# A decoder's wide attention: row maxima from bf16 copies of keys and queries instead of the fp32r parts

## The reference

```python
q = (x_normed @ w_q)              # 1024 x 1024, 16 heads of 64
k, v = split(ctx @ w_kv)          # 6404 x 1024 each
scores = einsum('bhqd,bhkd->bhqk', q, k) * 64 ** -0.5
out = einsum('bhqk,bhkd->bhqd', softmax(scores), v) @ w_out + b_out
```

## Time and profile before

| | |
|---|---|
| three timed runs | 3840.88, 3855.21, 3857.26 us, median 3855.21 |
| profiled execution, span from first to last instruction | 3852.1 us |
| PE, DVE, ACT, POOL busy | 93%, 71%, 56%, 61% |
| first part of the wide attention | about 1607 to 1664 us |
| its steps | from 1664 us to about 3667 us |
| time of the profiled execution beyond its span | not given by the page |

### The profile page before, as it was taken

The page is one execution under the profiler, slowest core; times in us unless marked ns, Lnnn a source line. Parts: engine busy times, 40 slices in busy tenths (PEclk is TensorE's granted clock), DMA queues, the critical chain, the costliest instruction groups (busy, mean ns, idle before and its releaser), DMA issues.

```text
span 3852.1 us, 61024 instructions
## 1 busy us (share of the span) xinstructions
PE 3585.8 (93%) x23264; PEld 1471.9 (38%) x23264; DVE 2721.2 (71%) x4447; ACT 2164.0 (56%) x2535; POOL 2367.2 (61%) x1280
## 2 busy tenths in 40 slices
PE   6868999999999999889999999999999999999999
PEld 2332222222222244334444444444444444444444
DVE  5758888888888547776766666667666676666742
ACT  4667888888888744644444444444444444444422
POOL 3115656566565303047888888888788888889810
PEclk7969999999999999999999999999999999999999
DMA  4220001010001002500111000101010010012100
GB/s 132 52 44 8 1 10 27 1 26 11 1 1 43 10 5 87 204 14 25 29 29 29 27 28 27 30 25 32 26 29 27 28 29 28 25 55 71 30 0 6
DMA packets 74058, 126.73 MB, mean 33 GB/s; under 512 B 9875, under 2 KB 26341, under 8 KB 73093
## 3 DMA queue, kind: packets, MB, share of 16 engines
q1 hardware_dynamic: 73772, 122.82, 11.2%
HBM read 88.15 MB, written 34.64 MB: 32 GB/s over the span
## 4 chain that ended last, share of the span: by engine, by line
PE 51%; DVE 4%; ACT 2%; issue 1%; DVEq 0%; ACTq 0%
PE PS L2371 20%; PE PS L2345 12%; PE PS L2300 6%; PE PS L2358 5%; PE PS L2318 3%; DVE att_top_piece L2555 2%; DVE att_k_lo L2569 2%; PE PS L340 1%; PE PS L348 1%; PE PS L341 1%; ACT att_k_hi L2463 1%; PE PS L2311 0%; PE PS L2329 0%; PE PS L2323 0%; DVE att_prob L2535 0%
## 5 line engine op out<-in xcount | busy, mean ns | idle before, releaser
L2220 POOL TENSOR_TENSOR att_total<-att_total,att_prob 128x1024 f32<-128x1024 f32 x597 | 1543.7, 2586 | 352.4 <-ACT att_prob L2484 304.5
L2484 ACT ACTIVATE att_prob<-PS 128x1024 f32<-128x1024 f32 x816 | 790.9, 1021 | 1005.1 <-PE PS L2358 1005.1
L2555 DVE TENSOR_REDUCE att_top_piece<-PS 128x1 f32<-128x512 f32 (+1 forms) x1560 | 971.8, 664 | 349.6 <-PE PS L2300 339.8
L1878 DVE TENSOR_REDUCE att_top_piece<-PS 128x1 f32<-128x512 f32 (+1 forms) x1459 | 904.9, 664 | 132.4 <-PE PS L1591 127.0
L1781 ACT ACTIVATE att_prob<-PS 128x1024 f32<-128x1024 f32 (+2 forms) x912 | 892.0, 1004 | 173.5 <-PE PS L1623 170.6
L2371 PE MATMUL PS<-att_prob,att_vals 128*64 128x512 f32 x3264 | 792.0, 605 | 3.7 <-issue 2.9
L1646 PE MATMUL PS<-att_prob,cross_Vst 128*32 128x256 f32 (+1 forms) x5544 | 506.5, 431 | 2.7 <-issue 0.8
L1493 POOL TENSOR_TENSOR att_stage<-att_stage,att_run 128x512 f32<-128x512 f32 x150 | 191.4, 1276 | 401.9 <-ACT att_stage L1760 401.6
L2300 PE MATMUL PS<-att_k_hi,att_q_hi 64*128 64x512 f32 (+1 forms) x1664 | 376.3, 449 | 60.3 <-DVE att_top_piece L2555 47.0
L1591 PE MATMUL PS<-cross_Kstack,cross_Qmax 49*128 49x512 bf16 (+1 forms) x1664 | 323.5, 386 | 95.1 <-DVE att_top_piece L1878 33.4
L2345 PE MATMUL PS<-att_q_hi,att_k_hi 64*128 64x512 f32 x1632 | 329.1, 396 | 0.0
(11 more groups left out here) (316 smaller groups left out, 3394.6 us busy)
## 6 DMA issues: line engine op xcount, KB each, us to landing
att_vals<-values SPq DMA_DIRECT2D x192, 256.0 KB, 2.6
values<-att_prob SPq DMA_DIRECT2D x14, 1024.0 KB, 4.1
values<-cross_Vall SPq DMA_DIRECT2D x10, 1024.0 KB, 4.2
cross_Kstack<-kparts SPq DMA_DIRECT2D x36, 204.0 KB
f_w<-in_f_w SPq DMA_DIRECT2D x24, 256.0 KB, 3.7
kparts<-cross_Vst SPq DMA_DIRECT2D x24, 128.0 KB, 1.8
att_vals<-values SPq DMA_DIRECT2D x16, 192.0 KB, 2.3
k_ctxT<-in_ctxT SPq DMA_DIRECT2D x1, 2448.0 KB
```

What stands on the lines that cost most here:

```text
L1878: dve.tensor_reduce(top_piece[:, n % 2, s * QT + qt, c:c + 1], PS[:, banks[item][s], 0:w], AX, ALU.max).then_inc(dve_freed, 1)
L2220: pool.tensor_tensor(so_far, so_far, prob[0:rows, j % RING, :, :], ALU.add).then_inc(summed, 1)
L2484: act.activation(prob[:, j % RING, :, :].rearrange("p a b -> p (a b)"), PSf[:, b:b + 2 * HALF], ACT.Exp, scale=scale).then_inc(exped, 1)
L2555: dve.tensor_reduce(top_piece[:, n % 2, s * QT + qt, c:c + 1], PS[:, bank_of(item, s), 0:w], AX, ALU.max).then_inc(dve_freed, 1)
```

## The change

Two tiles are added: `k_top`, bf16 copies of the 6404 keys of a pair, and `q_top`, bf16 copies of the queries of two units. ACT writes them from the same PSUM bank as the hi parts and ahead of these, with the same semaphore count behind both copies. The maxima matmuls read these tiles. The scores, the subtraction and all else are as before. The program is also built with a smaller scratch area for dynamic DMAs.

```diff
+        k_top, q_top = m.sb("k_top", [P, NCTX], BF16), m.sb("q_top", [P, 2, HALF], BF16)
...
                     for s in range(2):
-                        ins = pe.matmul(PS[:, bank_of(item, s), 0:w], q_hi[n % QBUFS][strip(s), qt * P:(qt + 1) * P],
-                                        k_hi[p % 2][strip(s), c * HALF:c * HALF + w], start=True, stop=True,
+                        ins = pe.matmul(PS[:, bank_of(item, s), 0:w], q_top[strip(s), n % 2, qt * P:(qt + 1) * P],
+                                        k_top[strip(s), c * HALF:c * HALF + w], start=True, stop=True,
                                         tile_position=(s * DH2, 0))
...
                 if kind == "q":
+                    act.activation(q_top[:, n % 2, :], PS[:, bank_of(item), :], ACT.Copy)
                     act.activation(q_hi[n % QBUFS][:, :], PS[:, bank_of(item), :], ACT.Copy).then_inc(hi_copied, 1)
                 elif kind == "k":
                     c = chunk(item[2])
+                    real = min(NCTX, c.stop) - c.start
+                    act.activation(k_top[:, c.start:c.start + real], PS[:, bank_of(item), 0:real], ACT.Copy)
                     act.activation(k_hi[n % 2][:, c], PS[:, bank_of(item), 0:c.stop - c.start], ACT.Copy
                                    ).then_inc(hi_copied, 1)
...
-    nc = bacc.Bacc("TRN2", target_bir_lowering=False, num_devices=1)
+    nc = bacc.Bacc("TRN2", target_bir_lowering=False, num_devices=1, dynamic_dma_scratch_size=1024)
```

## The result

| | median | runs |
|---|---|---|
| before | 3855.86 us | 14, 3840.88 to 3871.80 |
| changed kernel | 3874.57 us | 14, 3869.39 to 3884.24 |

The ratio is 1.0052, 95% interval 1.0039 to 1.0065: slower by 19 us, just over what one can tell from no change, and inside the predicted range, 12.6 us above the predicted 3862. The profiled execution has a span of 3872.9 us, 20.8 us more than before's.

What follows compares the result with a forecast made beforehand. The prediction took TensorE's own order to bound the steps of the wide attention. Its terms, 49.6 - 10.5 - 32.2 - 2.8 + 3 = +7 us, added to the median of 3855.2, gave 3862 us, range 3836 to 3905.

Steps and rivals of the forecast that it cites:

- Term 1: Steps, 105 fills: ACT's added copy delays hi copy, lo part, reduction and early pair by up to 0.48 us; +49.6 us.
- Term 2: Steps, early maxima pair after a fill's wait: cheaper bf16 weight load, 0.10 us off in 105 cases; -10.5 us.
- Term 3: Steps, late maxima pairs behind the values' matmuls: 0.11 us off each of 293 for the bf16 load; -32.2 us.
- Term 4: Steps, early maxima pairs without a wait: only the stream gets shorter, 0.01 us in 277 cases; -2.8 us.
- Term 5: First part: ACT becomes the bound at some 3.74 us a chunk against 3.54, in 12 chunks; +3 us.
- Rival A: Borders between fp32r and bf16 on PE stop loads running ahead; 90 us more, 3952 us; chance 0.17.
- Rival B: ACT's copy doesn't reach PE's wait after fills, so its 50 us go; 3812 us; chance 0.12.
- Rival C: Steps lose more, 0.60 us a copy instead of 0.48, with 6 in the first part; 3878 us; chance 0.13.

Runs made afterwards that it cites:

- reads_only: Changed kernel without the copies: the maxima matmuls read bf16 tiles that GpSimd set to zero once; ratio 0.9910 to the kernel before.
- pe_filled: Changed kernel with every maxima pair of the first part run twice into the same bank; 3867.55 us, ratio 1.0029 to the kernel before.
- scratch_only: Kernel before with only the smaller scratch area for dynamic DMAs; median 3859.87 us, ratio 1.0010.
- copies_only: Changed kernel with the bf16 copies written but read by nobody, the maxima matmuls reading fp32r parts; ratio 1.0165 to the kernel before.
- before_again: Kernel before, unaltered, profiled a second time; 3872.58 us.

## Why the prediction was right in its range and off in a term

- **Term 1** (+49.6, copies on the chain): shown. +50.0 when alone; 0.48 to 0.49 a fill; gone when the order is turned.
- **Terms 1 and 2 together**, +0.38 a fill: measured +0.380 (5.961 to 6.341) for keys and +0.383 for queries, 37.6 us in 105 fills against the 39.1 forecast. Term 2 alone, -0.10: reads_only has fills at 5.854, -0.107.
- **Term 3** (-32.2, late pairs): the size per pair was right, 4.350 to 4.246 and no more from the early pair, 0.104; the count was too high. I took 398 - 105 = 293 late pairs as if none stood twice in a double-step; only 273 double-steps without a fill have one or more, and the first and fourth lines of the table, 266 of them, gained 28.1 us. The estimate of 107 ns for an fp32r load doesn't hold, it is 184 ns; no term used it.
- **Term 4** (-2.8, early pairs): nothing. From the last scores to an early pair it is 238 ns instead of 230 by the starts of the trace, from there to the subtraction 320 instead of 327. The two cancel.
- Terms 1 to 4 gave +4 and measured +8.9; 3 and 4 are most of the difference.
- **Term 5** (+3, first part): this is the step that failed. It measured +11.7. It said that ACT would become the bound at 3.74 us a chunk, and took PE's 12.56 of 18 busy us as a sign that PE didn't matter. It left the granted clock out: with the copies there the clock is 0.50 in the chunks instead of 1.00, and at that clock PE's chunk is 4.70 us and the bound. pe_filled has the same copies at the full clock, at 3.75 us a chunk, and takes 58.5 and 59.1 us. Against first parts with the same clock at their start that is +3.5 (58.5 against the 55.0 of scratch_only, both at 1.00 from the start through the last chunk) and +2.4 (59.1 against 56.7, both at 0.50 in the first fills). So the forecast for ACT alone was right (+3), and the clock adds some 9 us (68.3 against 59.1 in the second profiles).
- **Rival A** (type changes cost PE): refuted, by the rows at the border and by reads_only.
- **Rival B** (the copy is covered): refuted by copies_only.
- **Rival C** (larger loss): its sum, 3878, came nearer to the measured 3874.57 than mine, but not by its mechanism: the steps lost 0.38 and not 0.50 a fill.
- **Sum.** 3855.9 + 8.9 + 11.7 = 3876.5 against 3874.57 measured.

What is shown is that the copies in the first part bring the half clock: it is there with them and gone without them, in the profiles and, but for the overlap, in the mean clock of the runs. What is not settled is how. That PE's idle time lets the clock fall is supported by pe_filled alone, where more work for PE and a shorter stand held it. The rows speak against any simple form of it: the kernel before holds 1.00 with a stand of 1.1 us in every chunk and PE busy for 12.56 of 18 us, reads_only with stands of 1.33 us and 11.33 of 18, while the change and copies_only stay at 0.50 with PE shown busy for 16.24 and 17.57 of 18. In copies_only and before_again the clock was down before the first chunk, behind the stand of 2.59 us that every kernel has there, and what was missing is the rise. What exactly is counted no run here shows.

## What to carry to other kernels

When a copy is added for a new reader, put it behind the result that others wait for, with a count of its own: in the steps the copies cost 50 us ahead of the hi part and nothing behind it, where they read the hi part in SBUF. (In the first part they brought the half clock in either place.) Look at who waits at the end of the chain before calling an engine idle: ACT was idle for 57% of the steps, and late in every fill. In a stretch where TensorE isn't the bound, ask what it would take at the half clock: if that is more than the present bound, as the 4.70 us a chunk were here against 3.54, a delay elsewhere can turn the stretch into a TensorE-bound one. And where one execution is compared with another, look at the granted clock of the stretch first: the same code took 56.7 and 69.6 us.

## What the runs showed of the hardware

- bf16 and fp32r matmuls of one tile shape follow one another without a gap, loads run ahead across the border (L2346's load 0.01 us behind L2301's), while a change of tile shape costs 0.10 us (0.33 us from early pair to subtraction against 0.23 from score pair to score pair).
- Behind such a change a bf16 pair is 0.10 to 0.11 us cheaper than an fp32r pair. The loads take 92 against 184 ns, which fits a load in the open; no run separates the two.
- Two ACT copies of 128x512 in a row are 0.48 to 0.50 us apart at 0.60 each.
- Adding matmuls made a stretch 9 to 10 us shorter, with the granted clock at 1.00 instead of 0.50.
- The same code ran a stretch at 1.00 or at 0.50 (before and before_again), and at 0.50 PE was shown busy for over 90% of it without a rise.
